# FFN and attention phases that alternate between two halves of the tokens, and a selective scan in batch-sized steps spread over the first two of them

## What is computed

```python
x = x + L0_xattn(ctx, layernorm(x), ...)   # selective scan over ctx (1024 x 128), gated by silu(layernorm(x))
x = x + L0_ffn(layernorm(x), ...)          # 32 experts, inner width 96, top 8 of each token, softmax weights
x = x + L1_xattn(layernorm(x), ctx, ...)   # 16 query heads, 8 key/value heads of 128, keys and values from ctx
x = x + L1_ffn(layernorm(x), ...)          # 16 experts, inner width 128, top 2, and two shared chunks
```

```python
state = state * exp(delta_t * A) + (delta_t * u_t) * B_t
y_t = sum_n(state * C_t)
```

## Time and profile before

| | |
|---|---|
| median of 3 runs | 811.45 us (811.41 to 813.08) |
| profiled execution | 812.3 us, its span 810.5 us |
| TensorE busy | 686.6 us (85%) |
| VectorE busy | 580.0 us (72%) |
| ScalarE busy | 435.8 us (54%) |
| POOL busy | 272.7 us (34%) |
| mean granted TensorE clock | 0.939 |

### The profile page before, as it was taken

The page is one execution under the profiler, slowest core; times in us unless marked ns, Lnnn a source line. Parts: engine busy times, 40 slices in busy tenths (PEclk is TensorE's granted clock), DMA queues, the critical chain, the costliest instruction groups (busy, mean ns, idle before and its releaser), DMA issues.

```text
span 810.5 us, 10345 instructions
## 1 busy us (share of the span) xinstructions
PE 686.6 (85%) x3520; PEld 558.4 (69%) x3520; DVE 580.0 (72%) x1077; ACT 435.8 (54%) x844; POOL 272.7 (34%) x259
## 2 busy tenths in 40 slices
PE   5266726586888899999989999999799898999997
PEld 1244514465666678888877999987698776888885
DVE  6999977799999856646457766676766385544454
ACT  4685525455552444545466777777577444333442
POOL 0200031122222423445445465644356342221221
PEclk8599885798889999999999999999999999999999
DMA  6357832454545415544311111100021232534240
GB/s 232 108 171 246 235 117 89 123 154 138 174 133 148 146 53 170 161 152 142 118 56 35 40 42 38 53 27 30 25 60 54 83 120 75 159 104 124 79 137 26
DMA packets 43989, 88.70 MB, mean 109 GB/s; under 512 B 6136, under 2 KB 8448, under 8 KB 43936
## 3 DMA queue, kind: packets, MB, share of 16 engines
q1 hardware_dynamic: 43936, 88.04, 35.8%
HBM read 82.44 MB, written 5.57 MB: 109 GB/s over the span
## 4 chain that ended last, share of the span: by engine, by line
PE 53%; DVE 16%; issue 9%; ACT 4%; DMA 1%; POOL 0%; SPq 0%; DVEq 0%; ACTq 0%
PE bank L86 17%; PE bank L87 16%; PE bank L88 16%; DVE read_out L1068 3%; PE bank L599 2%; ACT probs L910 2%; DVE bank L1211 2%; DVE state L1058 2%; DVE hidden_lo L960 1%; DVE scores L1322 1%; DVE head_out_lo L960 1%; DVE x_norm L991 1%; ACT head_out_hi L682 1%; DVE bank L1214 1%; DVE x_tok L1082 1%
## 5 line engine op out<-in xcount | busy, mean ns | idle before, releaser
L1395 POOL TENSOR_TENSOR w_lo<-w_raw,w_hi 128x768 fp32r<-128x768 f32 (+1 forms) x106 | 178.4, 1683 | 375.9 <-ACT w_hi L682 374.6
L86 PE MATMUL bank<-xt_hi,w_hi 128*128 128x512 f32 x400 | 166.0, 415 | 30.4 <-DVE hidden_lo L960 30.4
L88 PE MATMUL bank<-xt_hi,w_lo 128*128 128x512 f32 x400 | 161.9, 405 | 0.0
L87 PE MATMUL bank<-xt_lo,w_hi 128*128 128x512 f32 x400 | 161.9, 405 | 0.0
L682 ACT ACTIVATE w_hi<-w_raw 128x768 fp32r<-128x768 f32 (+1 forms) x106 | 82.3, 778 | 108.7 <-PE bank L88 102.3
L86 PEld LDWEIGHTS bank<-xt_hi,w_hi 128*128 128x128 f32 x400 | 77.4, 193 | 50.6 <-DVE hidden_lo L960 34.8
L682 ACT ACTIVATE hidden_hi<-bank 128x512 fp32r<-128x512 f32 x84 | 49.4, 588 | 113.1 <-DVE bank L1214 111.6
L960 DVE TENSOR_TENSOR hidden_lo<-bank,hidden_hi 128x512 fp32r<-128x512 f32 x84 | 57.7, 687 | 56.9 <-ACT hidden_hi L682 56.9
L1211 DVE TENSOR_TENSOR bank<-gated,bank 128x512 f32<-128x512 f32 x80 | 55.3, 692 | 51.8 <-PE bank L88 51.1
L88 PEld LDWEIGHTS bank<-xt_hi,w_lo 128*128 128x128 f32 x400 | 77.4, 194 | 19.2
L87 PEld LDWEIGHTS bank<-xt_lo,w_hi 128*128 128x128 f32 x400 | 77.5, 194 | 15.2
(11 more groups left out here) (166 smaller groups left out, 1351.3 us busy)
## 6 DMA issues: line engine op xcount, KB each, us to landing
w_raw<-in_ffn_w SPq DMA_DIRECT2D x74, 384.0 KB, 3.5
b_rows<-bc_scratch SPq DMA_DIRECT2D x32, 256.0 KB, 4.0
c_rows<-bc_scratch SPq DMA_DIRECT2D x32, 256.0 KB, 3.6
w_raw<-fold_scratch SPq DMA_DIRECT2D x32, 256.0 KB, 2.6
route_bc<-route_scratch SPq DMA_DIRECT2D x32, 256.0 KB, 3.6
route_bc<-route_scratch SPq DMA_DIRECT2D x32, 192.0 KB, 3.5
fold_scratch<-fold_sb SPq DMA_DIRECT2D x8, 512.0 KB, 4.7
route_bc<-route_scratch SPq DMA_DIRECT2D x32, 128.0 KB, 3.7
```

Of the source, the lines that this page charges most:

```text
L86: e.matmul(out, w_hi, m_hi, start=first, stop=False)
L87: e.matmul(out, w_hi, m_lo, start=False, stop=False)
L88: return e.matmul(out, w_lo, m_hi, start=False, stop=last)
L1395: e.tensor_tensor(lo[:, 0:n], w_raw[p % RAW][:, 0:n], hi[:, 0:n].bitcast(F32), ALU.subtract).then_inc(sem("w_lo"), 1)
```

## The change

The order is now: FFN 0 half 0 (24 units, `RUN1`), attention half 0 (32 head units), one run of FFN 0 half 1 (24 units) and the first 10 chunks of FFN 1 half 0 (to `RUN2`), attention half 1, one run of the last 8 chunks of FFN 1 half 0 and all 18 of half 1. FFN 1 half 0 is thereby in two parts; the first one's sum is added to x by an extra partial transition, 10 (copy, turn, add). No piece of weights serves two halves any more: FFN 1 loads and splits 36 pieces instead of 26. The table of pieces is computed from places in this order.

The scan has 64 steps of one batch (128 x 2 x 256) instead of 32 of two. B and C rows of a step come in one transfer, four buffers. Batches 0 and 1 are scanned before the FFN; of the other 32 half steps one stands before its first unit, 23 within the units of FFN 0 half 0, 8 within the first 16 units of attention half 0, behind which x of half 1 is gated, added, normalised and routed, still in attention. ScalarE computes decays three steps at a time after every third unit. Transition 4 stands between the first FFN run and attention by itself; transition 6 runs in the units of FFN 0 half 1, transition 5 in those of FFN 1 half 0 behind them. The weight passes of pieces 0 and 1 no longer wait for the folds, and one of them stands before the rstd of half 0, one behind it. Masked scores stay in their bank; the turn of the first routing matrix stands behind `gate_up(1)`.

```diff
-        units0 = [(c, h) for h in range(HALVES) for c in range(FFN0_CHUNKS)]
-        units1 = [(c, 0) for c in range(ALONE)]
...
+        units = [(0, c, 0) for c in range(FFN0_CHUNKS)]
+        RUN1 = len(units)
+        units += [(0, c, 1) for c in range(FFN0_CHUNKS)] + [(1, c, 0) for c in range(FIRST_PART)]
+        RUN2 = len(units)
+        units += [(1, c, 0) for c in range(FIRST_PART, FFN1_CHUNKS)] + [(1, c, 1) for c in range(FFN1_CHUNKS)]
...
+        split_in, at_place = {}, -1
+        for p in range(2, PIECES):
+            at_place = max(at_place + 1, freed_in[p - SPLIT] if p >= SPLIT else 0)
+            split_in[places[at_place]] = p
...
@@ vector
-                e.tensor_tensor(drive[i % 2][:, :, :], delta_u[:, h, :, :],
-                                b_rows[i % 3][:, :].unsqueeze(1).broadcast_to([P, EH, HT]),
+                e.tensor_tensor(drive[s % 2][:, :, :], delta_u[:, h, :, in_half(b)],
+                                bc_rows[s % ROWS][:, 0:1, :].broadcast_to([P, EH, SEQ]),
                                 ALU.mult).then_inc(sem("drive"), 1)
...
+            for u in range(RUN1):
+                s = HB * DS + 1 + u
                 multiply_hidden(u)
+                if u < RUN1 - 1:
+                    scan_state(s)
+                    scan_drive(s + 1)
                 rest_hidden(u)
+                if u < RUN1 - 1:
+                    scan_read(s)
...
+            for step in range(7):
+                transition(4, step)
+            for q in range(GROUP):
+                rest_projected(0, q)
+            attend(0)
...
@@ scalar, behind round_hidden(u) of the first run
+                if u % 3 == 0:
+                    for s in range(HB * DS + u + 3, HB * DS + u + 6):
+                        scan_decay(s)
...
@@ tensor
+            down(RUN1 - 2)
+            down(RUN1 - 1)
+            for step in (1, 2, 5, 6):
+                transition(4, step, (2, 3))
...
@@ scalar and tensor, attention
-                ps = take(4 + i % 2, ("masked", 2 * i + 2))
+                ps = take(4 + i % 2, ("exp", i + 1))
...
@@ gpsimd
+            scale_norm(0, "z0")
+            rest_weights(0)
+            scale_norm(0, 2)
+            rest_weights(1)
```

More of the change, by code:

```diff
@@ new lines, in build, with add_piece @@
+        places = []
+        for run in range(3):
+            places += [("unit", u) for u in range(run_starts[run], run_ends[run])]
+            if run < HALVES:
+                places += [("head", run, i) for i in range(HALF_UNITS + DRAIN)]
+        place_no = {where: n for n, where in enumerate(places)}
+        pieces, from_fold, piece_freed, needed_in, freed_in = [], [], [], [], []
+        piece_of, proj_piece, out_piece = {}, {}, {}
+        def add_piece(source, folded, freed, needed, done):
+            pieces.append(source)
+            from_fold.append(folded)
+            piece_freed.append(freed)
+            needed_in.append(place_no[needed])
+            freed_in.append(done)
+            return len(pieces) - 1
@@ L403, in turn_acc, with y_term @@
-            def turn_acc(k, pair, ring=(0, 1)):
-                at.wait_ge("acc_copy0", k - 3)
-                at.wait_ge("acc_copy1", k - 3)
-                ps = misc(("acc", k, pair), ("added", 2 * (k - 4) + pair + 1), ring)
+            def y_term(b, t, first, last):
+                ps = take(y_bank(b), ("y_added", b + 1)) if first else bank[y_bank(b)]
+                for l in range(SEQ // P):
+                    for c in range(EH):
+                        turned = e.matmul(ps[:, l * DI + c * P:l * DI + (c + 1) * P],
+                                          read_out[t % READS][:, c, l * P:(l + 1) * P], identity[:, :],
+                                          is_transpose=True, start=first and l + c == 0, stop=last and l + c == 2)
+                turned.then_inc(sem("y_sum"), 1)
@@ new lines, in y_skip, with y_read, turn_z @@
+            def y_skip(b):
+                at.wait_ge("skip", b + 1)
+                y_term(b, TERMS * b, True, False)
+            def y_read(s):
+                at.wait_ge("read", s + 1)
+                y_term(s // DS, term(s), False, s % DS == DS - 1)
+            def turn_z(b, z_bank):
+                at.wait_ge("z_norm", b // HB + 1)
+                ps = take(z_bank, ("z_gate", b + 1))
+                bank_of["z", b] = z_bank
+                for l in range(SEQ // P):
+                    for c in range(EH):
+                        last = e.transpose(ps[:, l * DI + c * P:l * DI + (c + 1) * P],
+                                           z_gate[:, b * EH + c, l * P:(l + 1) * P], identity[:, :])
+                last.then_inc(sem("z_turn"), 1)
@@ L659, in _ @@
+            down(RUN2 - 2)
+            for q in range(GROUP):
+                project(KV_HEADS, q, (q,))
+            down(RUN2 - 1)
+            attend(1)
+            for u in range(RUN2, UNITS):
+                n = u - RUN2
+                if n > 0:
+                    gate_up(u)
+                if n >= 2:
+                    down(u - 2)
                 if n < 2:
-                    transition(7, n + 1)
+                    transition(7, n + 1, (0, 1))
                 if n == 4:
-                    transition(7, 5)
```

1049 lines of the change are left out of this document (536 added, 513 removed).

## The result

The changed kernel takes 848.1 us (median of 4 runs, 845.2 to 849.3) where the kernel before, beside it on the same chip, takes 811.4 (4 runs, 811.3 to 813.1): ratio 1.044, 95% interval 1.041 to 1.047. It is 4.4% slower; 835.5 was forecast, in a range of 806 to 850. The profiled execution's span is 845.2 us, 34.7 more than before; the terms of the prediction give 24.0.

A forecast was written before the change was run, and what follows sets the result against it. VectorE was taken to bound the scan stages, TensorE the rest. Terms -9.5 + 11 + 16.5 + 2 + 4 = +24.0 on the profiled 812.3 us gave 836.3, with the median 0.85 lower: 835.5, range 806 to 850.

The forecast's parts named there:

- the second rival: First FFN phase: every POOL weight pass lands on a VectorE pass, pace 6.8 us per unit, +16: 851; chance 0.15.
- the rhythm of three: First FFN phase: hidden_lo units of 5.4 to 6.8 us, VectorE idle before a gated multiply after every sixth decay pass.
- The 24 units: First FFN phase: 23 units at 6.1 us take 140.3, plus 7 for moved work; 24th hidden_lo 9.5 us earlier.
- I take one and a half: First FFN phase: POOL weight passes on the path per three-unit loop, 1.41 us each, giving 6.1 us per unit.
- the extras: First FFN phase: statistics and z of half 1, context splits, mask, gate, add; 10 us on VectorE, 7 counted.
- To hidden_lo 0: Start to first hidden_lo: half steps cost more, moved statistics and earlier weight passes save; sum -5.6, at 147.6 us.
- a cover of 5.9: First scan: 5.9 us of VectorE work between a B/C row's release and next use, against loads landing in 4.0.
- Exposed transition: First FFN phase to first attention: a 9.2 us chain plus about 2 for half-clock TensorE, +11; bounds 0 to 14.
- Second drain and fill: FFN/attention boundaries: a boundary pair costs 16.4 us and now occurs twice, +16.5; bounds 10 and 17.
- Attention and FFN behind: Attention phases +2 (scan steps +6, second routing +9, partial sum +1.5, against 15.0 before); later FFN phases +4 for transitions.
- the third rival: First FFN phase: same loop, but POOL's weight passes fall beside it or start second; pace 5.4, -16: 820; chance 0.24.
- The second rule: ScalarE's table switches: 2.66 us each, the load and a drain of 1.38; fifteen switches would add another 21 us.

The follow-up runs named there:

- the best version: Kernel before, with POOL's rstd ahead of its first weight passes, read_out ahead of hidden_lo and POOL's weight pass waiting for read_out in scan units: 789.3 us, ratio 0.972.
- the other version: Kernel before, with POOL's rstd ahead of its first weight passes and the weights' low part on VectorE in units with scan: 801.7 us, ratio 0.988.

## Why the prediction was right, and where its sizes were off

**Direction and mechanism held, the sizes less so.** The forecast had the scan's gain in the first FFN phase, and an exposed transition, a second drain and fill and the rest against it; the sum came out at +34.7 instead of +24.0. The 848.1 us lie 12.6 above the forecast and 2.9 below the second rival's 851, near the upper end of the range. Of the signs named beforehand, the rhythm of three with VectorE's wait for gated came as described; the units are 6.9 and not 5.4 to 6.8, the first hidden_lo stands at 150.98 and not near 148, and TensorE is without work for 7.6 us at the boundary (0.88 + 5.28 + 1.46 in the rows above), where about 9 was said.

**The 24 units (forecast -9.5 at hidden_lo 23; measured +2.9).** This is the term that was mis-sized most. Its loop was right: 16.3 us per turn summed, 16.46 measured with the passes out. Wrong was "I take one and a half" for POOL's passes: all three meet a VectorE pass, one of them the scan. Three at 1.41 give 6.8 per unit, which is the second rival's condition and pace, and the steady turn has 6.9. So in this term it was the rival, given 0.15, that came true, and not the forecast. I had also read the trace of before wrongly, as "nearly every scan unit shows one such stretch": by the earlier trace rows two stretches fall in one unit and none in the one before, and every POOL pass there meets VectorE. The pace alone would add 16 us in 23 units; the stage took 9.0 more than forecast (156.3 against 140.3 + 7 for the extras). With POOL's passes out it takes 135.3 us, 9 more than 23 units of the steady 5.49: the extras are worth that much. In the changed kernel it takes 2.3 less than 23 units of 6.9, because between hidden_lo 6 and 9, where most of the extras stand, the narrow passes gain nothing: there POOL's passes were hardly on the path. That the mean over the stage is 6.80 too is chance.

**To hidden_lo 0 (forecast -5.6; measured -2.3).** The half steps are 2.32 us long and follow each other without a gap but for two waits. One is for rows of B and C. The other, 2.43 us at 78.66, is for TensorE, which stood behind a skip term that ScalarE computes only after two logarithms and two table loads; I had not followed this moved item through ScalarE's queue. How much of the 3.3 us missed is this wait can't be said from one trace: in the eight traces of kernels whose edits all lie behind hidden_lo 0 (the changed kernel's with them) the wait is 0.9 to 3.0 us and hidden_lo 0 stands at 149.6 to 153.6, not in the same order. The rows, costed at nothing, do land later than forecast:

```profile
bc_rows<-bc_scratch SPq DMA_DIRECT2D x64, 256.0 KB, 5.6
```

That is 5.6 us where it was 4.0 for b_rows and 3.6 for c_rows, and where I had a cover of 5.9. The page's own idle column has 0.5 us of named waits in 64 drives:

```profile
L1150 DVE TENSOR_TENSOR drive<-delta_u,bc_rows 128x512 f32<-128x512 f32 x64 | 58.7, 918 | 0.9 <-DMA bc_rows<-bc_scratch 0.5
```

These waits come to 0.4 to 1.7 us in the ten traces with the new order, so the zero held to within 2 us, with almost no cover left. Why the loads take longer (runs half as long, or two rows in one load among other traffic) was not tried.

**Exposed transition (forecast +11; measured 16.0 more between hidden_lo 23 and mask 0 than before).** That is outside the stated bounds (0 to 14). The run with the transition moved takes 13.1 of it away, which is inside them. From the end of ScalarE's copy (311.63) to that of the second xt_lo (322.41) the chain takes 10.8 us, where 9.2 were summed up; the last down at the lower clock adds 1.2. Of the 2.9 that stay, the run with two banks takes back 2.4: I had followed the chain to the first of the query products and no further. The first query's products at the lower clock lie in the same stretch (starts 0.43 us apart in place of 0.23), and their share was not separated.

**Second drain and fill (forecast +16.5; measured +15.5).** The other three boundaries take 14.7 + 7.5 + 18.1 = 40.3 us; the drain of before takes 17.3, and one attention unit and one FFN unit are in the new pair (7.4). That leaves 15.5. This term held, priced from before's own boundary.

**Attention and FFN behind (forecast +2 and +4; measured -1.8 and +2.2).** The scan steps cost 4.6 where I had 6, by a run of their own. The second routing's share I have not measured alone.

**The Trainium skill's two rules.** The first (SBUF — State Buffer, Who interferes with whom) says that the later of two colliding operations blocks. The traces agree on both sides: with POOL first the scan takes 2.32 instead of 1.22, and with VectorE's scan first (in the run with the decay block behind the gate) the scan keeps its 1.22 and a POOL pass takes longer than its 1.8:

```profile
222.69 1.22 DVE L1161 TENSOR_TENSOR_SCAN state<-decay_t,drive 128x512 f32<-128x512 f32 x1
223.82 2.28 DVE L1153 TENSOR_TENSOR drive<-delta_u,bc_rows 128x512 f32<-128x512 f32 x1
...
222.97 2.58 POOL L1542 TENSOR_TENSOR w_lo<-w_raw,w_hi 128x768 fp32r<-128x768 f32 x1 [4.40 <-ACT w_hi L755]
```

But the drive behind that scan now finds POOL's pass under way and takes 2.28 instead of 0.67. So the VectorE pass that started first lost nothing itself, and the next one with two inputs in SBUF paid instead: "start second" alone would not have given the third rival its pace of 5.4. In the turns shown above POOL came first each time. The same section says that a VectorE instruction with at most one SBUF input, outside its 2-port modes, doesn't contend, and the best version rests on that: 0.68 to 0.70 us beside a POOL pass of 1.83. I had read the section for the order only, and so counted collisions instead of asking where none can be. The second rule (ScalarE: Activation LUTs, What ACT_TABLE_LOAD costs) would have added 21 us for a drain. In the changed kernel too, gated starts 0.01 us behind its load of 1.28 (215.63, 216.92). Taking all sixteen loads out gave 2.84 us per turn, 1.42 for each, and 23 us in the phase (20.5 by the loads' own time), where 2.66 for each would give 43.

## What to carry to other kernels

When several engines run a software pipeline with in-order queues, sum up the loop through all of them, and place a fixed block on one engine where its own lead is large: of the two places tried, the same decay block cost 3.5 us per turn behind hidden_hi and nothing behind the gate. Before pricing how often a POOL pass collides with VectorE, look for a stretch of VectorE passes with a PSUM operand that is as long as the pass, and make POOL wait for its start: here that was worth 1.4 us per unit. A change of phase order should be costed with what it exposes at each new boundary; here they cost 31 us, as much as the scan phase gives back even when its loop is repaired.

## What was not expected of the hardware

- The scan instruction is stretched by a POOL pass as well: 2.32 us instead of 1.22 for 128x512 when the pass (1.80 us) began 0.56 us before it. Before, only drive and read had shown it.
- x_norm, with a single tensor operand (four passes of 128x256, all in SBUF), is stretched too: 5.39 us for three of its passes, where all four take 1.37. In both versions made from the kernel before, POOL's passes 0 to 3 stand behind rstd and run into it. In the best version rstd ends 4.9 us earlier than in the kernel before, but x_norm, 5.7 us for all four passes in place of 4.3, ends only 1.2 us earlier. hidden_lo 0 came 2.0 us earlier there and 3.4 in the other version, which has the same order up to that point; the rest of that is not explained. From the best version's trace:

```profile
116.20 5.39 DVE L991 TENSOR_SCALAR x_norm<-x_tok,mean_var,rstd 128x256 f32<-128x256 f32 x3
...
113.80 7.64 POOL L1395 TENSOR_TENSOR w_lo<-w_raw,w_hi 128x768 fp32r<-128x768 f32 x4
```

- The loads of B and C rows take 5.6 us instead of 4.0 and 3.6 to land, at the same size and number, with runs of 1 KB instead of 2 KB.
